# Low parts of expert weights from GpSimd to VectorE, and the end of an attention branch packed into fewer tiles

## What is computed

```python
def _L0_attn_ref(hidden_states, W_z, b_z, W_h, b_h, ln_w, ln_b, h0):
    k = hidden_states @ W_z.T + b_z
    log_z = -jax.nn.softplus(-k)
    log_coeffs = -jax.nn.softplus(k)
    log_tilde_h = _g_log(hidden_states @ W_h.T + b_h)
    ...
    a_star = jnp.pad(jnp.cumsum(log_coeffs, axis=-1), ((0, 0), (1, 0), (0, 0)))
    log_h = a_star + jax.lax.cumlogsumexp(log_values - a_star, axis=1)
    log_h = (log_h - log_h.mean()) / jnp.std(log_h, ddof=1)
    h = jnp.exp(log_h)[:, 1:, :]
    x = h + hidden_states
    mu = x.mean(axis=-1, keepdims=True)
    var = x.var(axis=-1, keepdims=True)
    return (x - mu) * jax.lax.rsqrt(var + LN_EPS) * ln_w + ln_b

def _L0_ffn_ref(hidden_states, w_gate, w1, w2, w3):
    ...
    for e in range(NUM_EXPERTS):
        expert_weight = jnp.sum(routing_weights * (selected_experts == e), axis=-1, keepdims=True)
        h = jax.nn.silu(x @ w1[e].T) * (x @ w3[e].T)
        out = out + h @ w2[e].T * expert_weight

x = L0_attn_hidden_states
xn = _layernorm(x, axis=-1)
x = x + _L0_attn_ref(xn, ...) + _L0_ffn_ref(xn, ...)
```

## Time and profile before

| | us |
|---|---|
| runs | 357.61, 359.3, 355.52 (median 357.61) |
| profiled execution | 357.79 |
| its span | 356.1 |
| TensorE busy | 325.8 (91%) |
| VectorE busy | 260.8 (73%) |
| ScalarE busy | 219.9 (62%) |
| GpSimd busy | 206.4 (58%) |
| granted TensorE clock, mean | 0.969 |

### The profile page before, as it was taken

One profiled execution on the slowest core, in us unless ns is written; L12 is line 12 of the kernel. 1 busy time (PEld: TensorE's weight loads), 2 busy tenths in 40 slices (PEclk: granted clock), 3 DMA queues, 4 the chain that ended last, 5 costly groups with the idle time before them and its releaser, 6 DMA issues.

```text
span 356.1 us, 6682 instructions
## 1 busy us (share of the span) xinstructions
PE 325.8 (91%) x1964; PEld 273.9 (77%) x1964; DVE 260.8 (73%) x466; ACT 219.9 (62%) x328; POOL 206.4 (58%) x137
## 2 busy tenths in 40 slices
PE   8998999799999999999898999999999999979830
PEld 8883464588878898997787899889898988969730
DVE  5488787989996899889899842584589668763300
ACT  2547997455879974999854269934853485323400
POOL 4500023159968674989899728563885475945331
PEclk9999969989999999999999999999999999999985
DMA  7924912005444542354354434542463534354621
GB/s 263 426 120 137 293 52 59 15 11 150 122 82 115 142 101 32 80 129 129 44 144 109 102 38 115 142 101 33 84 181 89 75 45 76 47 76 49 98 38 15
DMA packets 19086, 37.00 MB, mean 104 GB/s; under 512 B 2272, under 2 KB 13536, under 8 KB 19008
## 3 DMA queue, kind: packets, MB, share of 16 engines
q0 software_dynamic: 9168, 11.97, 21.5%
q1 hardware_dynamic: 8496, 22.56, 20.4%
q10 hardware_dynamic: 1376, 1.85, 1.4%
HBM read 27.45 MB, written 11.03 MB: 108 GB/s over the span
## 4 chain that ended last, share of the span: by engine, by line
PE 54%; DVE 23%; ACT 8%; issue 8%; DMA 2%; ACTq 1%; POOL 1%; POOLq 0%; DVEq 0%
PE PS L1296 23%; PE PS L1314 11%; PE PS L1190 6%; PE PS L1326 5%; DVE wrow L1067 3%; DVE tmp L961 3%; PE PS L1176 2%; DMA out<-work,sidx 2%; DVE hT L956 2%; DVE U L985 2%; DVE A L998 1%; PE PS L1220 1%; DVE xrow L1054 1%; DVE xrow L1059 1%; PE PS L1265 1%
## 5 line engine op out<-in xcount | busy, mean ns | idle before, releaser
L1296 PE MATMUL PS<-wbuf,xT 128*128 128x512 f32 (+1 forms) x648 | 149.6, 384 | 4.9 <-issue 3.7
L1296 PEld LDWEIGHTS PS<-wbuf,xT 128*128 128x128 f32 x648 | 118.3, 190 | 29.4 <-issue 9.3
L424 POOL TENSOR_TENSOR wbuf<-raw,wbuf x28 | 81.4, 2924 | 23.1 <-ACT wbuf L604 21.4
L406 POOL DMA_INDIRECT out<-work,sidx x35 | 62.7, 1792 | 53.2 <-ACT work L621 20.1
L1314 PE MATMUL PS<-wbuf,hT 128*128 128x256 f32 x648 | 86.8, 288 | 0.0
L1314 PEld LDWEIGHTS PS<-wbuf,hT 128*128 128x128 f32 x648 | 79.3, 189 | 1.9 <-issue 1.9
L390 POOL DMA_INDIRECT work<-xn_dram,gidx x39 | 50.4, 1292 | 51.8 <-DVE gidx L892 36.1
L595 ACT ACTIVATE tmp<-PS 128x512 f32<-128x512 f32 x72 | 32.0, 460 | 41.6 <-PE PS L1296 41.3
L961 DVE TENSOR_TENSOR tmp<-tmp,PS 128x512 f32<-128x512 f32 x72 | 35.0, 516 | 29.4 <-ACT tmp L595 28.6
L956 DVE TENSOR_TENSOR hT<-PS,hT 128x768 fp32r<-128x768 f32 x36 | 34.2, 949 | 29.3 <-ACT hT L590 24.2
L621 ACT ACTIVATE work<-PS,wrow 128x256 f32<-128x256 f32 x35 | 16.4, 470 | 38.0 <-PE PS L1314 38.0
(11 more groups left out here) (185 smaller groups left out, 350.7 us busy)
## 6 DMA issues: line engine op xcount, KB each, us to landing
raw<-w_main SPq DMA_DIRECT2D x24, 544.0 KB
raw<-w_main SPq DMA_DIRECT2D x8, 416.0 KB
xn_dram<-xrow SPq DMA_DIRECT2D x4, 516.0 KB, 7.2
out<-xrow POOLq DMA_DIRECT2D x4, 512.0 KB, 6.1
xrow<-x SPq DMA_DIRECT2D x4, 256.0 KB, 4.8
xrow<-x ACTq DMA_DIRECT2D x4, 256.0 KB, 5.4
small_sb<-small ACTq DMA_DIRECT2D x1, 768.0 KB, 7.9
work<-xn_dram,gidx POOLq DMA_INDIRECT x39
```

The source lines that it names most:

```text
L406: pool.indirect_dma_start(out, bass.IndirectOffsetOnAxis(sidx[:, j:j + 1], 0), ysb[:, j % DEEP, :], None, compute_op=ALU.add).then_inc(s_s ...
L424: pool.tensor_tensor(lo, raw[:, ds(part, WP)], hi.bitcast(fp32), ALU.subtract).then_inc(s_w, 1)
L1296: ins = pe.matmul(PS[:, at:at + cols], xT[:, slot, xpart, q * P:(q + 1) * P], wbuf[:, w, wpart, q * 2 * F + at:q * 2 * F + at + cols], sta ...
```

## The change

- The subtraction that makes the low part of a piece moves from POOL to VectorE: POOL has no `split_due` any more, and VectorE has it at the end of each tile, behind the hook `after(j)`, with the read of the plan, the branch and the loop.
- `AT` becomes (0, 1, 2, 3). The lines that count the plan stay, and so does the doubled count of the first entry of `AT[1:]`.
- `row_stats` of two pairs in each of tiles 20 to 23, one in `between` and one in `after`; `h_back` likewise, the second behind `h_tile`. One `row_deviations` for all rows in tile 24, one `row_scales` in tile 25, two `last_norm` in each of tiles 25 to 28.
- POOL issues the additions two by two, ahead of its tiles 28 and 30.

```diff
-AT = (0, 0, 1, 2)
+AT = (0, 1, 2, 3)
...
-            def add_attention(j, m):
-
-                pool.wait_ge(s_p2, 4 * m + 4)
-                rows_added(j, m)
-                pool.dma_start(out[4 * m * P:4 * (m + 1) * P, :].rearrange("(t p) d -> p t d", p=P),
-                               xn[:, 4 * m:4 * m + 4, :], accum_op=ALU.add).then_inc(s_ab, 16)
+            def add_attention(j, first):
+
+                pool.wait_ge(s_p2, 4 * first + 8)
+                rows_added(j, first)
+                for m in (first, first + 1):
+                    pool.dma_start(out[4 * m * P:4 * (m + 1) * P, :].rearrange("(t p) d -> p t d", p=P),
+                                   xn[:, 4 * m:4 * m + 4, :], accum_op=ALU.add).then_inc(s_ab, 16)
...
-                    if j in (27, 29, 31):
+                    if j in (28, 30):
                         add_attention(j - 1, added)
-                        added += 1
-                    done = tile(i, u, done, added)
-            add_attention(SURE - 1, added)
+                        added += 2
+                    tile(i, u, added)
...
-            def row_deviations(h):
-                act.wait_ge(s_p1, 3 * (4 * h + 4))
+            def row_deviations():
+                act.wait_ge(s_p1, 3 * NT // 2)
...
-                    elif j in (18, 24, 28):
+                    elif j in (18, 24):
...
+            def split_due(before, j):
+
+                done = dve.value_load(plan[0:1, ds(j + 1, 1)], min_val=0, max_val=PIECES * (E - 1))
+                with dve.If(before < done):
+                    with dve.Fori(before, done) as p:
+                        part = dve.snap(p % PIECES * WP)
+                        hold(dve, s_hi, p + (PIECES + 1))
+                        lo, hi = (wslot(p // PIECES + 1, n, part) for n in (1, 0))
+                        dve.tensor_tensor(lo, raw[:, ds(part, WP)], hi.bitcast(fp32), ALU.subtract).then_inc(s_w, 1)
+                return done
...
-                if 20 <= j <= 27:
-                    row_stats(j - 20)
+                if 20 <= j <= 23:
+                    row_stats(2 * (j - 20))
+                if j == 25:
+                    row_scales()
+                if 25 <= j <= 28:
+                    last_norm(2 * (j - 25))
...
-                if j in (25, 29):
-                    row_scales((j - 25) // 4)
-                if 25 <= j <= 32:
-                    last_norm(j - 25)
+                if 20 <= j <= 23:
+                    row_stats(2 * (j - 20) + 1)
+                if 25 <= j <= 28:
+                    last_norm(2 * (j - 25) + 1)
...
-                if 20 <= j <= 27:
-                    h_back(j - 20)
+                if 20 <= j <= 23:
+                    h_back(2 * (j - 20))
...
                 h_tile(j)
+                if hooks and 20 <= j <= 23:
+                    h_back(2 * (j - 20) + 1)
```

More of the change, by code:

```diff
@@ L1162, in tile @@
                     after(j)
+                if done is None:
+                    done = dve.value_load(plan[0:1, ds(j, 1)], min_val=0, max_val=PIECES * (E - 1))
+                return split_due(done, j)
             for i in range(8):
+                done = dve.value_load(plan[0:1, ds(LOOP * i + 1, 1)], min_val=0, max_val=PIECES * (E - 1))
                 for u in range(LOOP):
[L1166 removed]
+                    done = tile(i, u, done, True)
             tail(dve, tile)
```

35 lines of the change are left out of this document (10 added, 25 removed).

## The result

| | before | changed |
|---|---|---|
| median of the runs beside each other, us | 356.89 (355.52 to 359.3, 4 runs) | 363.21 (360.14 to 365.4, 4 runs) |
| profiled execution, its span, us | 357.79, 356.1 | 363.73, 361.9 |
| tile 9, 14, 20, 26, 33 starts, us | 133.65, 171.50, 217.15, 262.77, 315.85 | 136.39, 175.20, 221.91, 274.11, 325.33 |
| last scatter, us | 347.79 | 353.58 |
| VectorE, POOL busy, us | 260.8, 206.4 | 258.6, 124.3 |

What follows compares the result with a forecast made beforehand. TensorE's chain was taken to bound over half the span, VectorE's a quarter, POOL's queue the last 5 us. Tiles +0.6 and end -4.3 made -3.7 on the 356.1 span, 352.4, hence 354.0 us; range 349.5 to 360.5.

Steps and rivals of the forecast that it cites:

- L1067 back to 0.2 us, the subtraction at 1.28: VectorE's slot weight, 1003 ns mean beside POOL's subtractions, returns to 0.2 us; the moved subtraction takes near 1.28 us.
- The gate comes 0.5 + 1.2 = 1.7 behind the last high part: 1.1 us later where ACT is behind.: VectorE's gate products also wait for the piece: 0.5 us ahead of it, 1.2 for it.
- three limits: Each tile's time is the largest of ScalarE's sum, VectorE's sum and the room behind h_lo; tile 33 shifts +0.6 us.
- The slack w: VectorE work behind h_lo, hooks then pieces, is free up to 3.1 us before it delays the next tile.
- My own sum: Shifts of tile starts, tile group by tile group, with tile 26 put at +3.4 us and tile 33 at +0.6.
- Two row statistics in each of 20 to 23 fit: VectorE's work in those tiles, with two statistics of 1.66 us each and a piece, sums to 6.7 us.
- transposes neutral: Tiles 20 to 27: the statistics' transposes move ahead of later tiles' floor, no net cost; +1.8 us until there.
- The stretches that disappear: VectorE instructions lengthened beside POOL's subtractions become short, giving back time, such as 1.6 us in tiles 29 to 32.
- Additions, -4.3: End of kernel: POOL's paired additions let the last scatter wait only for its copy, 343.3 or 0.2 later against 347.79.
- register work on VectorE: Plan load, branch and loop on VectorE aren't hidden: 0.5 to 0.8 us in some 12 tiles, +9, thus 363; chance 0.15.
- POOL's transfers stopping the pieces: POOL's DMA instructions delay VectorE's subtractions, 1.0 to 1.6 us for some six, +3 to +6: 358 to 360; chance 0.1.
- The slack takes the wait (350): In the tiles the pieces' wait is absorbed and only shorter VectorE instructions count: 4 us more gained, 350; chance 0.2.

Runs made afterwards that it cites:

- Behind the gate: Pieces on VectorE, placed behind the next tile's gate products: against the kernel before, 351.6 us; with all parts and due tiles 0, 0, 1, 2, 348.68 us.
- the loop alone: Kernel before, pieces still on POOL; VectorE also runs plan load, branch, high-part wait and addresses, then copies one column: 360.28 us, ratio 1.0107.
- The handover version: Kernel before, but from tile 28 VectorE makes the pieces, with one more wait each; POOL makes them up to tile 27: 355.91 us, ratio 0.998.
- with the addresses ahead: Changed kernel, most of a piece's address computation moved ahead of its wait for the high part: 364.47 us, ratio 1.0222 against the kernel before.

## Why the prediction was wrong, point by point

- *L1067 back to 0.2 us, the subtraction at 1.28.* Right: 0.21 and 1.291. The price was right and the place was the error.
- *"The gate comes 0.5 + 1.2 = 1.7 behind the last high part: 1.1 us later where ACT is behind."* Right in kind: in tile 7 it is 126.31 - 124.40 = 1.91, so 1.38 later than the 0.53 that would be left without the piece. Between the high part's end and the piece it was 0.68 to 0.71 us in most pieces that waited, just above my bound of 0.66 from the earlier trace rows and above the 0.5 that I took.
- *How often it counts.* This is the step that failed. I counted the 1.1 in two tiles (of 19 to 21) and let tiles 5 to 13 and 24 to 27 absorb it as the largest of three limits: ScalarE's sum, VectorE's sum, and the slack w = 3.1 behind h_lo. These are not three limits beside each other. A gate that is late enough makes the hidden tile late, this h_hi on ScalarE, this the next high part and silu, and so the next gate: it is one loop, as the chain at tile 8 shows, and piece and address work lie on it. Tiles 6, 7 and 8 have distances of 1.74, 1.52 and 1.52 and take 0.78, 0.01 and 1.47 us longer than before; not every late gate counts, but far more than two did. By tile 14 that was +3.7 where I had +1.6, by tile 26 +11.3 where I had +3.4 (the row statistics, below, included). With only the engine changed, tile 33 was 4.7 us later; I had put +0.6 for the whole change. The slack w was of no use to the piece: in tiles 11, 20 and 25 it lies ahead of the high part's end, when the piece cannot start (3.09, 3.29 and 2.34 us), and in tiles 4 to 8 the attention branch's steps had used it up (in tile 7 until 124.31, 0.09 us ahead of the high part's end).
- *My own sum.* The terms that I gave up to tile 26 (+1.6, -1, +1.4, +1.8, +1.0) make +4.8, or about 0.9 less if the transposes of two tiles are given back by then; I wrote +3.4. And 2.2 + 3.4 + 0.2 + 1.2 is 7.0, not 7.2. Neither slip changes the direction, and neither makes up for +11.3.
- *"Two row statistics in each of 20 to 23 fit", "transposes neutral".* Wrong. Tile 20 took 11.19 us instead of 8.27. The gate comes 8.18 behind the tile's start instead of 6.26 (two pieces ahead of it); from the gate to the next tile it is 3.01 instead of 2.01, because the second transposes wait in TensorE's queue for the first pair's addition; and behind the waits of 2.03 and 0.54 us TensorE does much of the next up products at half clock:

```profile
230.83 0.87 PE L1330 MATMUL PS<-ident,tmp 128*128 128x128 f32 x6 [2.03 <-DVE tmp L944]
232.24 0.63 PE L1358 MATMUL PS<-ident,A 128*128 128x128 f32 x4 [0.54 <-DVE xrow L1020]
233.10 5.67 PE L1300 MATMUL PS<-wbuf,xT 128*128 128x512 f32 x18 [0.23 <-issue]
```

  Behind the gate the same pairs cost 9.27 in tile 20 (+1.0, the second transposes and their wait of 0.54), 2.4 us up to tile 25, and give 2.2 back between 25 and 29. In the changed kernel tiles 25 to 28 take 31.05 us instead of 28.54: the gates of tiles 25 and 26 stand 1.74 and 2.43 behind silu instead of 0.14 and 1.56 (tile 27 has 2.14 in both).
- *The stretches that disappear* I credited with several microseconds. With only the engine changed they bought nothing that shows, since the late gates took more. Behind the gate, tiles 0 to 32 are 4.7 us shorter than before, 1.56 of it the slow clock of tile 1; how much of the rest is the stretches is not told apart.
- *Additions, -4.3.* The size was right (31.94 to 28.25, -3.7), and the last scatter goes 0.8 us behind its data's end (352.78), as I had it. But moving the pieces alone gave -4.05 with additions one by one: where the tiles are late POOL's queue catches up by itself (27.89 there, 27.81 with only the due tiles changed). What the pairing itself is worth, about 3 us in the medians, shows only with the pieces behind the gate, where the tiles are early. I had credited one cause with what two did.
- *Rivals.* The first, register work on VectorE, gave the right time, 363, and is borne out in part: 0.68 to 0.71 us pass between high part and piece, most of it address work, and the loop alone cost 3.5 us in the tiles. But it counted a cost also in full tiles without a piece, such as 9 and 10. Its sign was to be gaps ahead of gates without a piece, in tiles 8 and 9. Tile 8 has a piece, and in tiles 9 and 10 there is no gap. One such gap does stand in tile 29, 1.70 us, and its cause wasn't looked for. And neither the place of the piece nor the packed end is in it, so that the time agrees is luck. POOL's transfers stopping the pieces: no piece of the changed kernel took over 1.294 us. The slack takes the wait (350): refuted here, and roughly what the other order reached (351.6 and 348.68). My list lacked the rival that two queues could share one order, high part then silu, piece then gate, though the earlier trace rows and the order of the code show it.
- *Weights needed two tiles later, zero.* True on VectorE within what can be measured (1.9 us with overlapping intervals); on POOL it costs 8 us by the medians, with an interval of 1.5 to 8.6.

## What to carry to other kernels

When work that waits for another engine is put in a queue, look at what the other engine does next and what the queue does next: if these are again producer and consumer, the wait and the work stand on the path in every round in which the producer is late, whatever the sums of busy time say. Put it behind the consumer of the next thing, where its input is long there: the same instructions took 361.27 us ahead of the gate and 348.68 behind it. And a delay may be taken as absorbed only after following it once around the loop to the same instruction.

## What the hardware showed beyond this

- TensorE's clock. In the changed kernel the granted clock is 1.00 from 224 to 233 us and 0.56 from 233.0 to 236.4, behind waits of 2.03 and 0.54 us; 18 up products then take 5.67 us instead of 4.11. From the view of windows (us, busy of each engine with its count, granted clock, transfers' share, GB/s):

```profile
230.00:233.00 3.00, 1.50 (x10) 1.06 (x10) 2.93 (x9) 2.99 (x5) 0.36 (x1) 1.00 0.89 258
233.00:236.40 3.40, 3.30 (x8) 2.61 (x9) 2.61 (x8) 3.07 (x3) 2.21 (x2) 0.56 0.69 158
```

  Of the two levels it is the lower one, 1.2 GHz, for most of that stretch, and this dip costs 1.56 us: here a late gate is paid for twice. It isn't always. In tile 3 of the changed kernel the up products take 5.66 us too, behind a wait of only 1.30 in tile 2, but those of tile 12 take 4.11, behind a wait of 2.10 in tile 11. The handover version shows it behind its wait of 3.24 us too (0.62 from 295.0 to 298.5). The version with all parts behind the gate has no such tile from tile 1 on.
- Where a piece on VectorE waits for its high part and nothing else holds VectorE up, it starts 0.68 to 0.71 us behind the end of it, 0.41 to 0.43 with the addresses ahead, and two waits in a row leave 0.83 us between two pieces (292.49 against 291.65).
